# A TensorE-bound attention and FFN kernel: the down weights laid out part by part, so that the down matmul reads one run of 512 columns

## The reference, cut to what matters

```python
Wg = dequant_nvfp4(gate_W_packed, gate_scales)   # [4096, 512]
Wu = dequant_nvfp4(up_W_packed, up_scales)       # [4096, 512]
Wd = dequant_nvfp4(down_W_packed, down_scales)   # [512, 4096]
gate = jnp.einsum('th,nh->tn', xt, Wg)
up = jnp.einsum('th,nh->tn', xt, Wu)
gelu = jnp.tanh(0.7978845608028654 * (gate + 0.044715 * gate ** 3)) * gate * 0.5 + gate * 0.5
inter = gelu * up
out = jnp.einsum('tn,hn->th', inter, Wd)         # the down product, 512 outputs
```

## Time and profile before

| | before |
|---|---|
| time, median of 3 runs | 2799.06 us (2796.89 to 2799.44) |
| span of the profiled execution | 2793.0 us |
| median less the span | 6.06 us |
| PE busy | 2661.9 us (95%) |
| DVE busy | 2176.9 us (78%) |
| ACT busy | 1226.9 us (44%) |
| POOL busy | 993.3 us (36%) |
| DMA in the FFN stage | 16 engines 68% busy, 254 GB/s |

### The profile page before, as it was taken

How to read it: one execution, slowest core, us unless ns; L and a number is a source line. 1 busy time by engine, 2 the same in 40 slices (tenths; PEclk the granted TensorE clock), 3 DMA queues, 4 the chain that set the end, 5 groups by cost and what they waited for, 6 DMA issues and landing times.

```text
span 2793.0 us, 54312 instructions
## 1 busy us (share of the span) xinstructions
PE 2661.9 (95%) x19200; PEld 2441.9 (87%) x19200; DVE 2176.9 (78%) x3724; ACT 1226.9 (44%) x2425; POOL 993.3 (36%) x1189
## 2 busy tenths in 40 slices
PE   5899989999799999999999999999999999999998
PEld 4787878888699999999999999999999999999998
DVE  6877787877578888888888888888888888755555
ACT  4444545445344444444444444444444444444443
POOL 3454444534324343433434353433344343200000
PEclk9999999999999999999999999999999999999999
DMA  3223223232776697678667766966786586657452
GB/s 117 90 87 102 88 99 98 87 104 76 283 270 237 221 360 264 222 267 318 243 242 297 275 242 235 365 235 225 264 340 239 211 338 256 248 199 288 182 202 76
DMA packets 197576, 599.87 MB, mean 215 GB/s; under 512 B 21224, under 2 KB 80488, under 8 KB 185200
## 3 DMA queue, kind: packets, MB, share of 16 engines
q1 hardware_dynamic: 162160, 496.89, 48.7%
q0 software_dynamic: 35328, 101.82, 9.8%
HBM read 417.83 MB, written 180.75 MB: 214 GB/s over the span
## 4 chain that ended last, share of the span: by engine, by line
PE 78%; DVE 15%; issue 4%; ACT 2%; POOL 0%; SPq 0%; DMA 0%; DVEq 0%; ACTq 0%; POOLq 0%
PE bank_a L881 22%; PE down L889 22%; PE bank_b L881 12%; PE proj L711 11%; PE bank_c L881 6%; DVE inter L1427 2%; DVE inter L1418 1%; PE scores L751 1%; DVE lut_line L1215 1%; PE pv L776 1%; PE scores L760 1%; DVE inter_parts L1434 1%; ACT inter L1128 1%; DVE probs L1308 1%; DVE hs L1242 1%
## 5 line engine op out<-in xcount | busy, mean ns | idle before, releaser
L881 PEld LDWEIGHTS bank_a<-h_in,gu_slot 128*128 128x128 f32 x6144 | 855.1, 190 | 70.7 <-ACT copy_p L1164 5.7
L881 PE MATMUL bank_a<-h_in,gu_slot 128*128 128x256 f32 x6144 | 898.2, 282 | 2.8 <-ACT copy_p L1164 2.8
L889 PE MATMUL down<-d_slot,inter_parts 128*128 128x512 f32 x3072 | 837.4, 394 | 2.0 <-DVE inter_parts L1434 2.0
L889 PEld LDWEIGHTS down<-d_slot,inter_parts 128*128 128x128 f32 x3072 | 529.0, 190 | 69.1 <-DVE inter_parts L1434 2.4
L881 PE MATMUL bank_b<-h_in,gu_slot 128*128 128x256 f32 x3072 | 456.5, 284 | 20.0 <-DVE up_val L1440 20.0
L592 POOL TENSOR_TENSOR lut_v<-lut_v,signed_scale 128x512 f32<-128x512 f32 x96 | 124.1, 1292 | 880.0 <-DVE lut_v L1231 880.0
L881 PEld LDWEIGHTS bank_b<-h_in,gu_slot 128*128 128x128 f32 x3072 | 404.4, 192 | 27.8 <-DVE up_val L1440 27.8
L1166 ACT ACTIVATE gate_val<-bank_a 128x256 f32<-128x256 f32 x256 | 98.1, 383 | 428.7 <-PE bank_a L881 428.7
L1414 DVE TENSOR_TENSOR up_val<-bank_b,copy_p 128x256 f32<-128x256 f32 x256 | 108.2, 423 | 206.0 <-PE bank_b L881 206.0
L1434 DVE TENSOR_TENSOR inter_parts<-inter,inter_parts 128x512 fp32r<-128x512 f32 x256 | 203.7, 796 | 33.7 <-ACT inter_parts L1132 33.7
L881 PE MATMUL bank_c<-h_in,gu_slot 128*128 128x256 f32 x1536 | 226.6, 284 | 0.0
(11 more groups left out here) (123 smaller groups left out, 3677.4 us busy)
## 6 DMA issues: line engine op xcount, KB each, us to landing
h_in<-h_scratch SPq DMA_DIRECT2D x64, 3584.0 KB, 12.9
acc<-out SPq DMA_DIRECT2D x64, 1024.0 KB, 5.4
out<-acc SPq DMA_DIRECT2D x64, 1024.0 KB, 4.3
gu_slot<-w_scratch SPq DMA_DIRECT2D x32, 1792.0 KB, 10.3
w_scratch<-w_parts POOLq DMA_DIRECT2D x96, 512.0 KB, 6.7
h_scratch<-h_out SPq DMA_DIRECT2D x32, 896.0 KB, 5.0
d_scratch<-w_parts POOLq DMA_DIRECT2D x32, 512.0 KB, 3.2
d_slot<-d_scratch SPq DMA_DIRECT2D x32, 512.0 KB, 16.9
```

Of the source, the lines that this page charges most:

```text
L881: ins = pe.matmul(bank[:, 0:HALF], lhsT, rhs, start=(start and n == 0), stop=(n == len(pairs) - 1), skip_group_check=True)
L889: ins = pe.matmul(down[tc][:].rearrange("p (k h) -> p k h", k=2), inter_parts[:, j % 2, u, tc * P:(tc + 1) * P], d_slot[j][:, :, v, :], st ...
```

## The change

The scratch tensor's order becomes row, hidden slot `n`, part `u`, output half `k`, column. The store of a half writes runs of 256 columns in place of 512, the load of a slot takes 4 KB of each row as before (rows now lie 8 KB apart in DRAM in place of 4 KB), and in `d_slot[j]` the high part of all 512 outputs lies in one run, the low part in the next. The matmul's moving operand and its output are written as one run of 512 columns.

```diff
-    d_scr = nc.dram_tensor("d_scratch", (NCP, 2, P, 2, 2, 256), F32, kind="Internal").ap()
+    d_scr = nc.dram_tensor("d_scratch", (NCP, P, 2, 2, 2, 256), F32, kind="Internal").ap()
@@
             def load_down(g, j):
-                sp.dma_start(d_slot[j][:].bitcast(F32), d_scr[g * GB + j // 2, j % 2]).then_inc(d_ld[j], 16)
+                sp.dma_start(d_slot[j][:].bitcast(F32), d_scr[g * GB + j // 2, :, j % 2]).then_inc(d_ld[j], 16)
@@
                 if k < 2:
                     split_store(c, k, s0 + 1, lut_v[:, row], w_parts[:, k],
-                                d_scr[c].rearrange("n p k u h -> p n k (u h)")[:, :, k], "p n u h -> p n (u h)")
+                                d_scr[c].rearrange("p n u k h -> p (n u) k h")[:, :, k], "p n u h -> p (n u) h")
@@
                 for m, (u, v) in enumerate(THREE):
-                    ins = pe.matmul(down[tc][:].rearrange("p (k h) -> p k h", k=2), inter_parts[:, j % 2, u, tc * P:(tc + 1) * P], d_slot[j][:, :, v, :],
+                    ins = pe.matmul(down[tc][:], inter_parts[:, j % 2, u, tc * P:(tc + 1) * P], d_slot[j][:, v].rearrange("p k h -> p (k h)"),
                                     start=(j == 0 and m == 0), stop=(j == NS - 1 and m == 2))
```

## The result

| | before | after |
|---|---|---|
| time, median of 4 runs each | 2798.46 us | 2811.86 us (2810.93 to 2812.79) |
| ratio of the times, with its interval | | 1.005 (1.0036 to 1.0065) |
| span of the profiled execution | 2793.0 us | 2810.6 us |
| mean granted TensorE clock | 0.990 | 0.988 |

The forecast was 2798.06 us in a range of 2787 to 2804, with 5% on slower. The time came out 13.8 us above the forecast and outside the range.

What follows compares the result with a forecast made beforehand. TensorE's matmul count times their spacing was taken as the bound. Matmuls -1.0 us, store, packets and load 0: span 2793.0 to 2792.0 us, plus 6.06 around it, gives 2798.06 us; range 2787 to 2804 us.

Steps and rivals of the forecast that it cites:

- The matmul's pattern: Down matmuls on TensorE: removing the jump between two runs gains 1 us, bounds 5.1 us gain to 2.6 us loss.
- (a): Down matmuls: the jump costs, one run takes 228 ns instead of 231.7; 11.4 us less, 2787.7 us; chance 8%.
- (b): Down matmuls: the jump explains all of 231.7 against the rule's 215.8 ns; 48.8 us less, 2750.2 us; chance 1%.
- (d): Matmul operand: already issued as one run, or still as two; time stays 2799.06 us; 5%, counted with "same".
- The store: GpSimd's down store, 512 pieces instead of 256: longer issue hidden, value 0, at worst 2.4 us.
- The addition that I priced: GpSimd's down store issue: 392 ns more for 256 more pieces, 12.5 us of GpSimd over 32 stores.
- The cover that I named: GpSimd in the FFN stage: its wait for VectorE's next unit, some 10 us each, hides the longer store issue.
- the cover were gone everywhere: GpSimd's 32 down stores: if no wait hid the longer issues, they would cost 12.5 us.
- Packets: DMA engines: 8192 packets more, at most 63 us per engine, nothing waiting soon for these stores; value 0.
- The load: Down slot load on SyncE: same 4 KB rows, now 8 KB apart; value 0, up to 4.7 us later costs nothing.
- the margin that I took for it: Slot 2's load: landed 22.1 us after issue, 4.7 us before its first use.
- (c): Down loads land late and TensorE waits ahead of slot 2; 2843 us if landing takes half as long again; chance 3%.

Runs made afterwards that it cites:

- run 2: Kernel after with the old store (2 KB pieces, old scratch order), each slot load split into two DMAs, flat matmul kept: ratio 0.9998, 2797.66 us.
- run 8: Kernel before with two small GpSimd DMAs in unit 3 of all 12 loop blocks, delaying the S1/S2 store about 1.15 us: ratio 1.0329, 2888.43 us.
- run 3: Kernel before with slot rows 8 KB apart in DRAM, 2 KB store pieces and two-run matmul kept: ratio 1.0001, 2798.31 us.
- run 9: Kernel after with SyncE's hidden-tile load issued about 1.5 us later: ratio 0.9999, 2797.26 us.
- run 7: Kernel after with GpSimd's packed and scales loads in unit 3 issued behind the S1/S2 store: ratio 1.0028, 2804.03 us.
- run 10: Kernel before with two small GpSimd DMAs in unit 3 of 12 blocks and the tile load about 1.5 us later: ratio 0.9995, 2796.89 us.

## Why the prediction was wrong

**The matmul's pattern** (-1.0 us). Right in kind and within its bounds: 0.69 and 1.39 us per piece after the earlier trace rows, and the ratio of 0.9998 in run 2. Rivals (a) and (b), with a gain from the flat run, fell with it. Rival (d) did too, since the operand's form changed to one run.

**The store** (value 0, bounds 0 to +2.4 us). This is the step that failed: the term put at 0, in the sentence "So the addition shortens a wait and moves no later GpSimd instruction". The addition that I priced, 392 ns an issue, did not even come: the issue grew by 6 ns. I had laid the 196 ns between a store of 128 and one of 256 pieces on the pieces, and doubled it. What differs between the two stores besides the pieces I can't tell; doubling the pieces showed that they are not it. The Trainium skill, "DMA: Bandwidth & Descriptors", section "Anatomy of one DMA — SWDGE (gpsimd) path", says that generating descriptors is a small cost and that many can be emitted before more of it shows. Row and rule agree here, 767 to 773 ns for twice the pieces, and I had not looked at the rule.

What came in its place I had left out: GpSimd stops for 1 us at intervals ahead of an issue, and the new pieces move those stops. Two of them fell ahead of the S1/S2 store, and the two stalls that they set off cost 7.5 and 8.1 us, 15.6 together, where the term said 0. They were in the trace of before, in the same list of waits as the earlier trace rows, each as a line of 1 us with no releaser; run by run they fell where nothing was near. Nor did I ask what stands close to the edge. The cover that I named is a mean of some 10 us over 78 waits. Unit 3 has 1.37 us between its store and the tile load, and a delay of about 1 us there costs 7.6, since it also lets the tile come sooner. The 12.5 us that I gave for "the cover were gone everywhere" was wrong in the same way. It counted the delay once at its own length, not what it sets off: run 8 has 8 x 1.11 + 4 x 1.76 = 15.9 us of delay on GpSimd and 91.7 us in the time.

**Packets.** I put 8192 packets more; the queue has 35328, exactly as before. What this view calls a packet is not a piece of 1 KB: most of the queue's packets (24576) have 4096 bytes in either trace. The share of 9.8% is also unchanged, so the zero was right, for another reason.

**The load** (0). Right in the time: over the whole run the load of a slot lands in 15.6 us after 16.9, TensorE has no wait at it, and run 3 shows that the pitch costs nothing. But the margin that I took for it shrank. The latest slot 2 of after, issued at 2304.05 us, lands 25.7 us later, at 2329.75:

```profile
DMA to landing us min/median/max: 25.7/25.7/25.7
2330.91 0.86 PE L889 MATMUL down<-d_slot,inter_parts 128*128 128x512 f32 x3
```

That leaves 1.2 us of the 4.7. Slot 2 takes at most 23.4 us in the trace of before, and at most 23.0 to 24.4 in the others with the old rows (run 8 aside), against 24.5 to 25.7 in those with the new pitch; single executions can't say that the pitch does it. Rival (c) named a late transfer as the way to a slower kernel, which is the kind of thing that happened, but the wrong one: the store of other weights, in a unit that the diff does not touch, had 1.4 us.

**The chances.** 5% for slower rested on (c) and on the ends of small sums. A change that alters what a queue does ahead of other work needed a rival for "a transfer trades places with another", priced with the stall and the clock behind it.

## What to carry to other kernels

Where two queues share the DMA engines, look up for each small store that an engine soon waits for how far ahead of the next large load it is issued; this distance, and not the mean wait, says what a delay costs. Before calling an engine's work hidden, list its shortest covers, its waits without a releaser among them, and ask what each would be if it were a microsecond later. To mend such a place, move the large load, as in run 9; it cost nothing here, while moving GpSimd's own instructions did (run 7).

## What the runs showed of the hardware

- GpSimd's queue pauses ahead of an issue. Ahead of a load, where it is not idle otherwise, these pauses took 0.99 to 1.2 us (0.76 to 0.77 in runs 8 and 10). Ahead of a store, where some 0.8 us of idleness is usual, the idle time was 1.0 to 2.4 us in all; 2.4 us was seen at down stores in 1 KB pieces (after), in 2 KB pieces (run 8) and at a `w_scratch` store (run 7). Mostly they came every 62 to 74 of its DMAs, and at the same DMAs in both traces of the kernel after, and in before and runs 2 and 3. Their place moved with the pieces of a store and with one DMA of 16-byte rows; two loads of 1 KB rows moved none of those after 1050 us.
- A store of 0.5 MB landed 12.8 us after its issue when 3.5 MB on another queue had been issued 0.2 us ahead of it, against some 3 us when issued 1.4 us ahead and 3.6 us when issued 0.48 us ahead (run 10). At the 344 GB/s that the windows show from 1361 to 1374 us, equal shares of the bytes would have it through in about 2 x 0.52 MB / 344 GB/s = 3 us. The Trainium skill, "DMA: Bandwidth & Descriptors", section "Queues, rings and completion order", has each engine take turns between its queues, packet by packet. The trace agrees: its packet records have 4096 bytes for the store and 28672 for the tile, and from 1366.07 us to the tile's last packets the 16 engines start 16 of the one and 16 of the other about every 1.2 us. Equal turns thus give the store an eighth of the bytes, and the whole of both, 4.2 MB, takes 12.2 us at 344 GB/s. Before its first packet 48 of the tile's 128 had started, and its last 48 came behind the tile; why it began so late no run shows.
- A 5.3 us idle time of TensorE was followed by matmuls at the 1.2 GHz level (1.45 us for six in place of 0.71) until about 1383 us; with the shorter waits in that stretch this added 2.2 us to it.
